# Second expert layer of a macaron block: the high and low halves of W2 as two 128-column matmuls into the same PSUM columns, added once by VectorE

## What is computed

```python
def _L0_ffn_ref(x, W1, b1, W2, b2):          # x is layer-normed
    x_flat = x.reshape(-1, d)                # d = 128, dff = 512, E = 8
    h = jnp.mod(x_flat[:, :TOP_K].sum(axis=1).astype(jnp.int32), E)
    sel = jnp.stack([h, jnp.mod(h + 1, E)], axis=1)
    def step(acc, params):
        e, W1e, b1e, W2e, b2e = params
        w = jnp.any(sel == e, axis=1).astype(x.dtype) / TOP_K
        y = jnp.maximum(x_flat @ W1e + b1e, 0.0) @ W2e + b2e
        return (acc + w[:, None] * y, None)
    ...
x = x + 0.5 * _L0_ffn_ref(_layernorm(x), ...)
x = x + _L0_attn_ref(_layernorm(x), ...)
x = x + 0.5 * _L0_ffn_ref(_layernorm(x), ...)
```

## Time and profile before

| | |
|---|---|
| median of 3 runs | 759.11 us |
| all runs | 755.38, 759.11, 761.88 us |
| profiled execution: span, first to last instruction | 753.1 us |
| profiled execution: its own time | no other than the span is given |
| busy PE (matmul), PEld (weight load) | 581.2 us (77%), 478.7 us (64%) |
| busy DVE, ACT, POOL | 548.3 us (73%), 427.6 us (57%), 486.8 us (65%) |
| mean granted TensorE clock | 0.948 |

### The profile page before, as it was taken

One profiled execution on the slowest core, in us unless ns is written; L12 is line 12 of the kernel. 1 busy time (PEld: TensorE's weight loads), 2 busy tenths in 40 slices (PEclk: granted clock), 3 DMA queues, 4 the chain that ended last, 5 costly groups with the idle time before them and its releaser, 6 DMA issues.

```text
span 753.1 us, 17637 instructions
## 1 busy us (share of the span) xinstructions
PE 581.2 (77%) x5204; PEld 478.7 (64%) x5205; DVE 548.3 (73%) x1249; ACT 427.6 (57%) x914; POOL 486.8 (65%) x502
## 2 busy tenths in 40 slices
PE   1179998778878887794799589998778787797882
PEld 0045896667767676681477445897667676686771
DVE  6897986767777667684775795986767676676772
ACT  2461776565665575570898101876565666476560
POOL 1295777777777777772026454777777777777772
PEclk9967999999999999997999879999999999999997
DMA  9991111111111111116202621111111111111110
GB/s 255 304 165 26 35 37 35 35 39 38 33 39 35 32 26 32 32 35 166 59 1 58 139 32 29 30 37 32 39 39 35 38 31 39 35 36 27 23 36 1
DMA packets 46386, 41.29 MB, mean 55 GB/s; under 512 B 6477, under 2 KB 39603, under 8 KB 46354
## 3 DMA queue, kind: packets, MB, share of 16 engines
q1 hardware_dynamic: 35346, 21.63, 12.6%
q0 software_dynamic: 9984, 18.81, 10.4%
q10 hardware_dynamic: 1024, 0.44, 0.3%
HBM read 23.93 MB, written 18.74 MB: 57 GB/s over the span
## 4 chain that ended last, share of the span: by engine, by line
POOL 34%; issue 28%; PE 21%; DMA 6%; DVE 4%; ACT 4%; POOLq 2%; SPq 1%; ACTq 0%; DVEq 0%
POOL G L492 12%; POOL x1d L499 10%; POOL out L499 9%; PE ps L681 4%; PE ps L706 3%; DMA w2r<-in_L_ffn_W 2%; POOL staged L519 2%; PE ps L742 2%; PE ps L798 2%; PE ps L799 2%; PE ps L724 1%; DMA X<-in_L_attn_x 1%; PE ps L726 1%; PE ps L725 1%; ACT h L596 1%
## 5 line engine op out<-in xcount | busy, mean ns | idle before, releaser
L596 ACT ACTIVATE h<-ps,b1t 128x256 f32<-128x256 f32 x624 | 244.5, 475 | 165.9 <-PE ps L726 165.8
L492 POOL DMA_INDIRECT G<-rows,staged x128 | 192.0, 1500 | 72.7 <-POOL staged L519 53.2
L742 PE MATMUL ps<-w2s,hhi 128*128 x1248 | 226.8, 276 | 0.7 <-DVE hlo L978 0.7
L744 PE MATMUL ps<-w2s,hlo 128*128 x1248 | 218.5, 221 | 0.0
L724 PE MATMUL ps<-xhi,w1s 128*128 128x256 f16 x624 | 172.2, 276 | 29.0 <-issue 26.2
L725 PE MATMUL ps<-xlo,w1s 128*128 128x256 f16 x624 | 171.6, 275 | 0.0
L726 PE MATMUL ps<-xhi,w1s 128*128 128x256 f16 x624 | 171.3, 275 | 0.0
L742 PEld LDWEIGHTS ps<-w2s,hhi 128*128 128x128 f16 x1248 | 123.5, 99 | 15.7 <-issue 1.1
L967 DVE TENSOR_SCALAR xn<-G 128x128 f32<-128x128 f32 x156 | 49.4, 370 | 108.8 <-DMA G<-rows,staged 107.8
L744 PEld LDWEIGHTS ps<-w2s,hlo 128*128 128x128 f16 x1248 | 123.6, 99 | 1.7
L978 DVE TENSOR_TENSOR hlo<-h,hhi 128x1024 f16<-128x1024 f32 x78 | 95.0, 1218 | 4.1 <-ACT hhi L614 4.1
(11 more groups left out here) (218 smaller groups left out, 798.5 us busy)
## 6 DMA issues: line engine op xcount, KB each, us to landing
rows<-X SPq DMA_DIRECT2D x2, 2080.0 KB, 20.6
rows<-X SPq DMA_DIRECT2D x4, 1040.0 KB, 7.4
X<-in_L_attn_x SPq DMA_DIRECT2D x8, 512.0 KB, 8.3
X<-x1d SPq DMA_DIRECT2D x8, 512.0 KB, 7.1
w1r<-in_L_ffn_W SPq DMA_DIRECT2D x1, 2048.0 KB, 11.0
G<-rows,staged POOLq DMA_INDIRECT x128
x1d<-O,staged POOLq DMA_INDIRECT x64
out<-O,staged POOLq DMA_INDIRECT x64
```

What stands on the lines that cost most here:

```text
L492: nc.gpsimd.indirect_dma_start(out=G[tile.slot][:, s, :], out_offset=None, in_=rows, in_offset=bass.IndirectOffsetOnAxis(ap=idx[:, s:s + 1 ...
L596: ins = nc.scalar.activation(h32[e][:, c, :], H[e][:, c, :], ACT.Relu, bias=bias[:, c:c + 1])
L742: nc.tensor.matmul(Y[tile.k][:, s, :], hhi[tile.k][e][:, c, tok], w, start=first, stop=False, skip_group_check=True)
L744: ins = nc.tensor.matmul(Y[tile.k][:, s, 0:P], hlo[tile.k][e][:, c, tok], wh, start=False, stop=(e == 1 and c == CH - 1), skip_group_check ...
```

## The change

The layer-2 matmul of 256 columns becomes two of 128 columns over the same stationary chunk, one with the high and one with the low half of W2. Both write to the same 128 PSUM columns, as the third one (hlo) does. Y needs 256 columns of its bank instead of 512. VectorE adds once, and `y_half` is gone.

```diff
-        Y = [ps[:, 4 + k, :].rearrange("p (s n) -> p s n", s=SUB) for k in range(2)]
+        Y = [ps[:, 4 + k, 0:FT].rearrange("p (s n) -> p s n", s=SUB) for k in range(2)]
...
-        y_half = sem("y_half")
...
                     for c in range(CH):
-                        w = w2v[:, bass.ds(held[tile.off][e] + c * 2 * P, 2 * P)]
                         wh = w2v[:, bass.ds(held[tile.off][e] + c * 2 * P, P)]
+                        wl = w2v[:, bass.ds(held[tile.off][e] + c * 2 * P + P, P)]
                         for s in range(SUB):
                             tok = slice(s * P, (s + 1) * P)
                             first = e == 0 and c == 0 and s == 0
-                            nc.tensor.matmul(Y[tile.k][:, s, :], hhi[tile.k][e][:, c, tok], w,
-                                             start=first, stop=False, skip_group_check=True)
-                            ins = nc.tensor.matmul(Y[tile.k][:, s, 0:P], hlo[tile.k][e][:, c, tok], wh, start=False,
+                            o = Y[tile.k][:, s, :]
+                            nc.tensor.matmul(o, hhi[tile.k][e][:, c, tok], wh, start=first, stop=False, skip_group_check=True)
+                            nc.tensor.matmul(o, hhi[tile.k][e][:, c, tok], wl, start=False, stop=False, skip_group_check=True)
+                            ins = nc.tensor.matmul(o, hlo[tile.k][e][:, c, tok], wh, start=False,
                                                    stop=(e == 1 and c == CH - 1), skip_group_check=True)
...
                         dve.wait_ge(y_ready, prev.done())
-                        v.scalar_tensor_tensor(out=o, in0=Y[prev.k][:, :, 0:P], scalar=scl[:, 2:3], in1=o, op0=ALU.mult,
-                                               op1=ALU.add).then_inc(y_half, 1)
-                        dve.wait_ge(y_half, prev.done())
-                        v.scalar_tensor_tensor(out=o, in0=Y[prev.k][:, :, P:2 * P], scalar=scl[:, 2:3], in1=o,
-                                               op0=ALU.mult, op1=ALU.add).then_inc(o_ready, 1)
+                        v.scalar_tensor_tensor(out=o, in0=Y[prev.k], scalar=scl[:, 2:3], in1=o, op0=ALU.mult,
+                                               op1=ALU.add).then_inc(o_ready, 1)
```

## The result

The changed kernel took 773.64 us (median of 4 runs, 769.82 to 799.75) beside 760.5 us of the kernel before on the same chip (median of 4, 755.38 to 764.91). The ratio is 1.016, with an interval of 1.0102 to 1.0217: slower by 1 to 2%, where 730 us had been predicted. The profiled execution has a span of 773.9 us against 753.1, so 20.8 us are to be found.

The account below looks back on a forecast made before the run. GpSimd (POOL), its gathers held by VectorE, was taken to set the 7.2 us tile period. Savings of 24.0, 4.3 and 1.0 us, 29.3 together, gave a span of 723.8, plus 6.0 for the median: 730 us, range 719 to 750.

Parts of the forecast that it names:

- Point 1: VectorE in each tile, L1019 to L978: one addition in place of two lets L978 start 0.51 us earlier.
- Point 2: GpSimd's gathers in a loop tile: earlier L978 and L999 let them end sooner, period 6.68 us instead of 7.19.
- the tile at 674.73: A traced tile where L978 started 0.16 us after the copy instead of 0.45; it took 6.90 us against 7.19.
- the slope of one: GpSimd's tile period shortens by as much as L978 comes earlier: 0.29 us less for 0.29 earlier.
- the sum: Whole kernel: 24.0, 4.3 and 1.0 us saved, together 29.3 us of the 753.1 us span.
- Point 3: Every fourth tile, where TensorE stands 1.78 us at L724 for its table load: the 0.51 us was taken as gained.
- Point 4: TensorE: three 128-column matmuls per group take 0.165 us as now; eight more register instructions per tile also add nothing.
- The rival on the slower side: TensorE: 128-column matmuls with new weight loads don't keep 0.055 us; 774 us at 0.077, 856 at 0.10; chance 0.08.
- The rival "hidden": VectorE: the merged addition only makes it idle 0.51 us more at L967; 758 us, chance 0.08.
- The 1.0 us per tile that TensorE had to spare: TensorE's loop tile: 7.19 less 5.71 us, less 1.78 / 4 for the table load; 0.06 us more per group costs nothing.

Follow-up runs that it names:

- The first experiment: The kernel before with VectorE's second addition (L1022) and its wait left out, TensorE untouched, so the low half is never added: 767.3 us, ratio 0.9967.

## Why the prediction was wrong

Two steps failed, one in each half of the change: VectorE's half was to give 29 us and gave nothing (0.9967), and TensorE's half was to cost nothing and cost 17 us (1.0221).

- Point 1, 0.51 us less of VectorE between L1019 and L978: right. L1019 starts at 584.37, L978 at 584.77, 0.40 us on.
- Point 2, what it does to POOL: the step that failed first, and on it all of the gain stood. It followed L978 to "0.06 us before the copy" and looked only at the gathers. The COPY is held by L978 in the same way as a gather is: 0.22 us became 0.93. What the gathers gained (21.2 us) the copies and scatters took (25.4), and the tile at 674.73, on which the slope of one rested, was the last point of the old regime: there L978 still came behind the copy. The first experiment measured this part at 0.9967 where the sum had put 29.3 us, 0.96. With the copy off GpSimd the half microsecond was worth nothing either; there TensorE's stalls stand against it (44 in that trace), so the held copy has not been tested by itself.
- Point 3, the fourth tile: wrong in sign. Its table load was taken as fixed at 1.78 us. In the changed kernel the idle time ahead of L723 there, over the seven edges inside each loop, averages 2.34 and 2.24 us against 1.61 and 1.77 ahead of L724 before, and it reaches 2.86 us at the first edge inside the loop. That is some 10 us in all, a term that the sum did not have.
- Point 4, spacing: right. The starts lie 0.055 us apart over whole runs, into the same columns, with a load in front of each. By the Trainium skill (TensorE: Matmul & The Clock Gate, section Back-to-back issue gap) 81 ns per matmul would have stood there; the trace shows 0.05 to 0.06 and doesn't agree.
- Point 4, "the eight more register instructions run on the sequencer ahead; I take nothing": the step that set the sign. They alone cost 0.6% (1.0064). The added loads and matmuls were likewise put at nothing beyond their spacing. The terms were 0 and measured 2.2% together (TensorE's half alone, 1.0221), or +17 us: stalls, longer table loads and time at the lower clock. How the 17 us are shared between addresses and matmuls no run resolves.
- The rival on the slower side named 774 to 856 us with "128-column matmuls don't keep 0.055 us". Its 774 matches the time and not the mechanism: they do keep it, and the stream that feeds them is interrupted. The rival "hidden" (758) gives the time of VectorE's half, but not its mechanism: VectorE's idle time at L967 did not grow, it fell from 108.8 to 93.6 us, and grew at the cast (23.0 to 53.2) and at L978 (4.1 to 22.1).
- The 1.0 us per tile that TensorE had to spare was taken as a cushion. The staged copy on VectorE points to part of it being in use: without it the unchanged stream of before stalls for 35 us in place of none.

What is shown: each half's effect; that the added instructions cost by stalls, longer table loads and the lower clock and not by spacing; that the stalls come with four indirect DMAs per tile and go with two, and are not gone with four at the bytes of two (one trace); that they remain with a loop of half the length. It was not tried to gather with plain DMAs from another queue, nor were instructions and packets of an indirect DMA told apart. Why the fifth and ninth tile are hit hardest is open too; every kernel with all of TensorE's half, four tiles per pass and GpSimd's copy in place shows it in stage 1 (10.0 to 10.8 and 12.5 to 13.1 us).

## What to carry to other kernels

An engine's idle time may be where its instruction stream catches up: before spending it on more and smaller instructions, look in the timeline for gaps released by "issue" in the middle of a group, and count what each edit adds to the stream, addresses included. Set the bound of such a count above the regular spacing at the lower clock, or steps of a slow clock are taken for gaps. When a chain of holds is shortened on one side, move every instruction of the other engine through the new times, the small ones too: a 0.2 us copy was held like the gathers. And splitting a change into its halves at once showed that the half with the gain gained nothing, while the half taken as free cost 2%.

## What the runs showed of the hardware

- TensorE's matmuls stop with nothing awaited, mostly 0.3 to 0.75 us from start to start, up to 47 times in 31 tiles of the changed kernel, while GpSimd issues four indirect DMAs per tile; with two there was no stop in 31 tiles, in either kernel.
- After such stops and long table loads the granted clock fell to 0.50 for some microseconds, and two tiles per stage took 10 to 15 us instead of 7. In stage 2 of the changed kernel the windows from 528 us on read:

```profile
528.00:532.00 4.00, 2.57 (x33) 2.16 (x30) 0.58 (x4) 0.92 (x1) 2.56 (x5) 1.00 0.16 49
532.00:536.00 4.00, 2.82 (x16) 1.22 (x14) 2.37 (x5) 1.84 (x5) 3.09 (x4) 0.74 0.13 33
536.00:544.00 8.00, 6.02 (x41) 4.78 (x40) 3.59 (x7) 2.77 (x6) 6.25 (x6) 0.50 0.13 41
544.00:552.00 8.00, 8.00 (x110) 7.61 (x109) 5.47 (x11) 6.08 (x15) 3.13 (x4) 0.99 0.05 17
```

  In 8 us at 0.50, stalls included, TensorE did 41 matmuls and in the next 8 us at 0.99 it did 110.
- A gather of 64 rows takes GpSimd nearly as long as one of 128. The shortest in stage 2, as a line's group (ns min/median/max), first of the kernel with half the rows, then of the changed kernel, whose median has more held gathers in it:

```profile
L492 POOL DMA_INDIRECT G<-rows,staged x64: 923/959/2257, 521.2 to 756.3; - x64
```

```profile
L491 POOL DMA_INDIRECT G<-rows,staged x64: 974/1182/2569, 509.2 to 740.2; - x64
```
